# Attention's layer norm folded into centred query weights and a variance term, x brought in already transposed, and the opening in another order

## The chip, the cores and the metric
The kernel runs on one core of one Trainium2 chip. The metric is the device time in microseconds (us) of one execution; the time shown is the median of three runs. Engines are called as in the profile: PE is TensorE (PEld its weight loads), DVE is VectorE, ACT is ScalarE, POOL is GpSimd, SP issues DMAs.

## The reference
`x` is 4 batches of 512 tokens of width 512, the context as large. The attention has 32 heads of width 16, and each head's query and key are RMS-normed. The expert part has seven routed experts (two for each token) and a shared one.

```python
def _layernorm(x):                       # eps = 1e-5
    return (x - mean(x)) / sqrt(var(x) + eps)
q = _layernorm(x) @ Wq.T                 # 32 heads of 16
k, v = context @ Wk.T, context @ Wv.T    # rows interleaved in the reference
q, k = q * rsqrt(mean(q*q) + 1e-6), k * rsqrt(mean(k*k) + 1e-6)      # per head
x = x + softmax(q @ k.T / 4) @ v
x = x + experts(_layernorm(x))
```

## The kernel before
There are two blocks. The first is attention, with the second layer norm and the router's products beside it; the second is the expert part, over tiles of 256 tokens. Only the first is changed.

**Tiling.** Attention is worked in 16 units: 4 batches times 4 groups of 128 columns (8 heads). In code `u = 4 * b + g`. A unit has 8 steps: two halves of its heads (`ab`) times four tiles of 128 keys (`mt`). In a step PE makes the scores of four heads by 512 queries (`scored`, L322, four PSUM banks), ACT takes the exponential of all 2048 columns (L646), and PE weighs the values with it (`weighed`, L338). `scores` has one buffer, so the scores of a step wait for the exponential of the step before. Between the scores of step s and the weighing of step s-1, PE has other work that `between(u, s)` lists: the k projection of unit u+1 and u+2, the q projection of unit u+2, one 512-column group of v of the next batch (`v_all`), the head sums of squares (`sum_q`, `sum_k`, with the 0/1 matrix `blocks`), and transposes.

**Precision.** Each projection is done as three fp32r matmuls, high by high, high by low, low by high. So every operand is split: high is a copy to fp32r, low the difference. `weight_low`, `weight_split`, `context_split` and the functions for `xt` do this.

**The first layer norm.** For each tile of 128 tokens DVE takes mean and variance (`stat`, L668), POOL takes (variance + eps) to the power -0.5 (`root`, L181) and normalises the tile (`norm`, L211), PE transposes it (`four_transposes`, L405), and ACT and DVE split the transposed tile into `xt_hi` and `xt_lo` (L522, L705, L722, L723). Columns of `xt` are tokens, so q needs all four tiles. For a following batch these steps stand in groups 1 and 2: transposes of tile 0 and 1 in steps 5 and 6 of group 1, of tile 2 in step 0 and tile 3 in step 2 of group 2. In the first batch DVE normalises (L928) and the transposes go to the idle `scores` banks.

**The RMS norm.** DVE adds 16 * 1e-6 to the head sums (`sums_q` L752, `sums_k` L758), ACT takes log and exp(-0.5 *), DVE and POOL refine with one Newton step, and DVE stacks the result in pairs of heads (`stack_q` L794 to L796, `stack_k` L801 to L804).

**Order.** Every engine has its own queue, written out by hand. Three PSUM banks are shared out in a fixed order that the function `uses` writes down: `bank_a` (k, some v), `bank_b` (q, some v) and `tr` (sums, transposes, router). `begin` waits until DVE has read the bank's use before. DVE's order of a step is in `step(u, s)`, ACT's in `before_exp(u, s)`.

**Opening.** SP loads four tiles of x, then k's group 0, the context, q's group 0, v, and the rest. PE does half of k(0), 16 transposes, the rest of k(0), its sum, q(0), v(0,0), sum_q(0), v(0,1), v(0,3), q(1), five turns of k(1) and sum_q(1), then the first scores.

Of the kernel before, what the change touches and what calls it, by code (L numbers as in the profile page):

```python
# [12 lines left out]
P = 128  # L13


def moe_layer(nc, x, ctx_t, wq_t, wk_t, wv_t, w_all, b_up_gate, b_down, w_router, b_router, gate_bias, xn_dram,
# [20 lines left out]
    with ExitStack() as ctx:  # L37
# [49 lines left out]
        twin_hi = asb("twin_hi", [P, SEQ], FP32R)  # L87
# [5 lines left out]
        blocks = asb("blocks", [P, P])  # L93
        lower, sign = asb("lower", [P, 1]), asb("sign", [P, 1])
# [6 lines left out]
        x_first = [sem(f"x_first{t}") for t in range(BT)]  # L101
# [9 lines left out]
        xn_ready, first_t, xt_high, xt_split = (sem(n) for n in ("xn_ready", "first_t", "xt_high", "xt_split"))  # L111
# [26 lines left out]
        def uses(bank):  # L138
            order = {"a": [("k", 0), ("k", 1)], "b": [("q", 0), ("q", 1), ("v", 0, 2)],
                     "tr": [("sum_k", 0), ("sum_q", 0), ("sum_q", 1)]}[bank]  # L140
            for u in range(UNITS):
                b, g, more, behind = batch_of(u)
                ahead = u + 2 < UNITS
                if bank == "a":
                    order += [("v", b + 1, 2 * g - 3)] * (more and g >= 2) + [("t", b + 1, 0)] * (more and g == 1)
# [3 lines left out]
                else:  # L149
                    order += [("t", b + 1, 2)] * (more and g == 2) + [("l", b - 1, 2)] * (behind and g == 3)  # L150
                    order += [("out", u - 1, 1)] * (u > 0)
                    order += [("sum_k", u + 1)] * (u + 1 < UNITS) + [("t", b + 1, 3)] * (more and g == 2)
# [18 lines left out]
        def _(pool):  # L171
# [10 lines left out]

            nc.gpsimd.memset(blocks[:], 1.0).then_inc(blocks_set, 1)
# [19 lines left out]
            def norm(b, i):  # L203
                if i == 0:
                    pool.wait_ge(rsqrt_ready, (1, 2, 3, 5)[b])
                    pool.wait_ge(mean_ready, (1, 2, 3, 5)[b])
                elif i == 2:
                    pool.wait_ge(a_ready, A_AT["t", b, 0] + 1)
                elif i == 3:
                    pool.wait_ge(tr_ready, TR_AT["t", b, 1] + 1)  # L210
                nc.gpsimd.tensor_scalar(xn[:, i % 2, :], x_sb[:, tile_of(b, i), :], mv[:, i, 0:1], rsqrt[:, 0, i:i + 1],  # L211
                                        ALU.subtract, ALU.mult).then_inc(xn_ready, 1)

            def norm2(b, i):
                if i == 0:
                    pool.wait_ge(rsqrt_ready, (4, 6, 7)[b])
# [6 lines left out]
            root(0, 0)  # L223
# [3 lines left out]
            roots = 1  # L227
            for u in range(UNITS):
                b, g, more, behind = batch_of(u)
                if more and g == 1:  # L230
                    norm(b + 1, 0)
                    norm(b + 1, 1)
# [3 lines left out]
                if behind and g == 1:  # L236
                    root(roots, 1)
                    roots += 1
                    norm2(b - 1, 0)
                    norm2(b - 1, 1)  # L240
# [3 lines left out]
                if more and g == 1:  # L244
                    norm(b + 1, 2)
                    norm(b + 1, 3)
# [3 lines left out]
                if u == 0 or (g == GROUPS - 1 and b + 2 < BATCH):  # L250
                    root(roots, 0)
                    roots += 1

        @block.sync
        def _(sp):
# [20 lines left out]
            load_context(1)  # L276
            sp.wait_ge(zeros_set, 1)
            zeros = xt2[:, 1].rearrange("p c n -> p (c n)").unsqueeze(1)
            for rows, width in ((xn_dram, D), (out, D), (xn_dram[:, D:], WIDE - D)):
                spare = rows[TOKENS:, 0:width].rearrange("(s p) d -> p s d", p=P)  # L280
                sp.dma_start(spare, zeros[:, :, 0:width].to_broadcast([P, 2, width])).then_inc(y_filled, 16)
            for b in range(1, BATCH):
                sp.wait_ge(ctx_split, (b + 1) * MT)
                if b + 1 < BATCH:
                    load_context(b + 1)
                else:
# [4 lines left out]
                for i in range(BT):  # L291
                    t = tile_of(b - 1, i)
# [8 lines left out]
        def _(pe):  # L301
# [8 lines left out]
            def scored(u, s):  # L310
# [4 lines left out]
                if t:  # L315
                    pe.wait_ge(p_ready, t)
                else:
                    pe.wait_ge(v_ready, MT - 1)
                for part in (k_hi, k_lo):
# [31 lines left out]
            def q_turns(u, first, end):  # L351
                g = u % GROUPS
                if first == 0:
                    begin("b", B_AT, ("q", u), b_free)
                    pe.wait_ge(w_split, W_AT[f"q{g}"] + 1)
                    pe.wait_ge(xt_split, (u // GROUPS + 1) * BT)
                for c, a, b in TURNS[first:end]:
                    last = nc.tensor.matmul(bank_b[:], (wq_hi, wq_lo)[a][:, g, c, :], (xt_hi, xt_lo)[b][:, c, :],
# [5 lines left out]
            def k_turns(u, first, end):  # L364
                g = u % GROUPS
                if first == 0:
                    begin("a", A_AT, ("k", u), a_free)
                    pe.wait_ge(w_split, W_AT[f"k{g}"] + 1)
                    pe.wait_ge(ctx_split, (u // GROUPS + 1) * MT)
                for c, a, b in TURNS[first:end]:  # L370
                    last = nc.tensor.matmul(bank_a[:], (wk_hi, wk_lo)[a][:, g, c, :], (ctx_hi, ctx_lo)[b][:, c, :],
# [5 lines left out]
            def v_all(at, b, mt):  # L377
                pe.wait_ge(w_split, W_AT["v"] + 1)
                pe.wait_ge(ctx_split, b * MT + mt + 1)
# [28 lines left out]
            def norm_transposes(b, i):  # L408
                if i:
                    begin("tr", TR_AT, ("t", b, i), tr_free)  # L410
                    at, ready = tr, tr_ready
                else:
                    begin("a", A_AT, ("t", b, i), a_free)
                    at, ready = bank_a, a_ready
# [1265 lines left out]
```

## Time and profile before
| what | us |
|---|---|
| median of three runs (1018.45 to 1020.17) | 1018.86 |
| profiled execution, its own time | 1018.88 |
| its span | 1017.1 |
| PE busy | 960.4 |
| DVE busy | 703.6 |
| ACT busy | 498.4 |
| POOL busy | 230.6 |

The span is from the first to the last instruction of the profiled execution. Busy times overlap between engines. A matmul's end is modelled and matmuls are pipelined, so the distance between two starts tells more of PE's pace than a duration. In a timeline a row's bracket is the idle time of its engine just before it, and what ended it.

### The profile page before, as it was taken

How to read it: one execution, taken by the hardware profiler on the slowest of the kernel's cores; microseconds unless marked ns; L12 is line 12 of the kernel's file. 1: busy time of each engine (PE TensorE's matmuls, PEld its weight loads, DVE VectorE, ACT ScalarE, POOL GpSimd, SP SyncE). 2: the span in 40 equal slices, each digit the busy share in tenths (PEclk: the TensorE clock that was granted, in tenths of full speed). 3: DMA queues.
4: the chain of work that ended last, by engine and by line, in shares of the span. 5: the costliest groups of instructions: out<-in, count | busy, mean ns of one | idle time of the engine just before them, and what ended most of it. 6: DMA issues, size and time to landing. Idle time of an engine off the chain costs nothing.

```text
span 1017.1 us, 18058 instructions
## 1 busy us (share of the span) xinstructions
PE 960.4 (94%) x6730; PEld 698.0 (69%) x6731; DVE 703.6 (69%) x1442; ACT 498.4 (49%) x614; POOL 230.6 (23%) x223
## 2 busy tenths in 40 slices
PE   3999999999999999985999999999999999999995
PEld 3634443454444554332999999899998998999995
DVE  5788767876688657764579775765857677757653
ACT  3577668855786658875233222422424243424211
POOL 1122012420132201321000000232333332333321
PEclk9999999999999999998799999999999999999998
DMA  9100100010000100301341214363363535544523
GB/s 342 73 1 2 42 1 1 22 64 1 1 2 21 63 1 1 105 21 42 99 153 55 72 46 183 74 190 59 74 186 73 175 64 168 167 108 111 144 56 41
DMA packets 28985, 78.94 MB, mean 78 GB/s; under 512 B 7040, under 2 KB 7040, under 8 KB 24832
## 3 DMA queue, kind: packets, MB, share of 16 engines
q1 hardware_dynamic: 18400, 52.31, 14.4%
q0 software_dynamic: 10528, 25.87, 12.8%
q8 instruction: 36, 0.59, 0.2%
q14 instruction: 21, 0.17, 0.1%
HBM read 57.64 MB, written 20.52 MB: 77 GB/s over the span
## 4 chain that ended last, share of the span: by engine, by line
PE 49%; DVE 2%; issue 1%; DVEq 0%; POOL 0%; ACT 0%; POOLq 0%
PE u_ps L1188 16%; PE z_ps L1188 15%; PE y_ps L1188 15%; PE xt_ps L1201 2%; PE z_ps L1182 1%; DVE w_sb L1390 1%; PE y_ps L1214 0%; DVE stats L1406 0%; DVE u_lo L1551 0%; DVE x_lo L1400 0%; DVEq L1032 0%; DVE y_sb L1579 0%; POOL out L1132 0%; PE xt_ps L1174 0%; ACT u_hi L1322 0%
## 5 line engine op out<-in xcount | busy, mean ns | idle before, releaser
L646 ACT ACTIVATE probs<-scores 128x2048 f32<-128x2048 f32 x128 | 240.6, 1879 | 75.8 <-PE scores L322 72.8
L1188 PE MATMUL u_ps<-x_hi,w_sb 128*128 128x256 f32 x896 | 167.9, 285 | 5.2 <-issue 3.0
L1188 PE MATMUL z_ps<-u_hi,w_sb 128*128 128x256 f32 x896 | 169.1, 287 | 0.2 <-DVE u_lo L1551 0.2
L1188 PEld LDWEIGHTS u_ps<-x_hi,w_sb 128*128 128x128 f32 x896 | 143.1, 194 | 8.0 <-issue 4.6
L1322 ACT ACTIVATE u_hi<-u_ps,b_ug 128x256 fp32r<-128x256 f32 x112 | 47.0, 471 | 204.0 <-PE u_ps L1188 204.0
L1188 PEld LDWEIGHTS z_ps<-u_hi,w_sb 128*128 128x128 f32 x896 | 142.4, 193 | 0.4 <-DVE u_lo L1551 0.4
L1188 PE MATMUL y_ps<-w_sb,g_hi 128*128 128x512 f32 x448 | 138.8, 391 | 0.4 <-DVE g_lo L1569 0.4
L338 PE MATMUL o_ps<-probs,v_sb 128*17 128x512 f32 x1024 | 134.8, 598 | 1.0 <-ACT probs L646 1.0
L1188 PE MATMUL u_ps<-x_lo,w_sb 128*128 128x256 f32 x448 | 127.7, 285 | 0.0
L1188 PE MATMUL z_ps<-u_lo,w_sb 128*128 128x256 f32 x448 | 127.2, 284 | 0.0
L1551 DVE SCALAR_TENSOR_TENSOR u_lo<-u_ps,b_ug,u_hi 128x256 fp32r<-128x256 f32 x112 | 49.0, 479 | 80.7 <-ACT u_hi L1322 80.0
L322 PEld LDWEIGHTS scores<-q_st,k_hi 32*128 32x128 f32 x512 | 24.6, 181 | 112.6 <-ACT probs L646 67.8
L1334 ACT ACTIVATE s_sb<-z_ps,b_ug 128x256 f32<-128x256 f32 x112 | 47.0, 471 | 104.0 <-PE z_ps L1188 103.9
L1188 PEld LDWEIGHTS y_ps<-w_sb,g_hi 128*128 128x128 f32 x448 | 82.3, 188 | 16.3 <-issue 0.5
L1132 POOL DMA_INDIRECT out<-y_sb,target x42 | 69.3, 1650 | 101.7 <-DVE y_sb L1586 92.2
L1188 PEld LDWEIGHTS u_ps<-x_lo,w_sb 128*128 128x128 f32 x448 | 86.9, 194 | 0.9
L1188 PE MATMUL y_ps<-w_sb,g_lo 128*128 128x512 f32 x224 | 87.2, 389 | 0.0
L1188 PEld LDWEIGHTS z_ps<-u_lo,w_sb 128*128 128x128 f32 x448 | 86.4, 193 | 0.0
L1564 DVE SCALAR_TENSOR_TENSOR g_sb<-u_ps,b_ug,s_sb 128x256 f32<-128x256 f32 x112 | 53.8, 481 | 31.7 <-ACT s_sb L1334 31.5
L322 PE MATMUL scores<-q_st,k_hi 32*128 32x512 f32 x512 | 64.6, 494 | 7.1 <-ACT probs L646 6.8
L1308 ACT ACTIVATE w_sb<-w_raw 128x1024 fp32r<-128x1024 f32 x48 | 48.1, 1060 | 31.0 <-PE y_ps L1188 28.3
L1579 DVE TENSOR_TENSOR y_sb<-y_ps,bd 128x512 f32<-128x512 f32 x56 | 38.4, 685 | 29.2 <-PE y_ps L1188 29.1
(218 smaller groups left out, 1585.5 us busy)
## 6 DMA issues: line engine op xcount, KB each, us to landing
w_raw<-w_all SPq DMA_DIRECT2D x27, 1024.0 KB, 7.0
ctx_raw<-ctx_t SPq DMA_DIRECT2D x4, 1024.0 KB, 6.8
out<-x_sb SPq DMA_DIRECT2D x16, 256.0 KB, 2.0
xg<-xn_dram POOLq DMA_DIRECT2D x14, 256.0 KB, 3.1
x_sb<-x SPq DMA_DIRECT2D x1, 3072.0 KB, 18.1
xn_dram<-xn SPq DMA_DIRECT2D x12, 256.0 KB, 2.1
bd<-b_down SPq DMA_DIRECT2D x9, 256.0 KB, 4.2
x_sb<-x SPq DMA_DIRECT2D x4, 256.0 KB, 3.7
```

What stands on the lines that cost most here:

```text
L322: last = nc.tensor.matmul(scores[:, j, :], part[rows, u % 2, ab, mt * P:(mt + 1) * P], q_st[rows, u % 2, ab, :], start=(part is k_hi), sto ...
L338: last = nc.tensor.matmul(o_ps[32 * j:32 * j + HD + 1, :], v_sb[b % 2][:, mt, head, :], probs[:, t % 2, j, :], start=(mt == 0), stop=(mt = ...
L646: nc.scalar.activation(probs[:, t % 2], scores[:], ACT.Exp).then_inc(p_ready, 1)
L1132: nc.gpsimd.indirect_dma_start(out=out, in_=y_sb[:, h, :], in_offset=None, compute_op=ALU.add, out_offset=bass.IndirectOffsetOnAxis(ap=tar ...
L1188: ins = nc.tensor.matmul(out_ps, stat[a], mov[b], start=(first and a + b == 0), stop=(last and a == 1), skip_group_check=True)
L1201: last = nc.tensor.transpose(xt_ps[:, b, a, h * P:(h + 1) * P], xg[:, h, c * P:(c + 1) * P], ident[:])
L1308: nc.scalar.activation(w_sb[:, par, 0, m, two], w_raw[:, m, two], ACT.Copy).then_inc(hi_done, 1)
L1322: last = nc.scalar.activation(u_hi[:, c, :], u_ps[:, b, a, :], ACT.Identity, bias=b_ug[:, par, 0, c:c + 1])
L1334: nc.scalar.activation(s_sb[:, c, :], z_ps[:, b, a, :], ACT.Silu, bias=b_ug[:, par, 1, c:c + 1]).then_inc(s_done, 1)
L1551: nc.vector.scalar_tensor_tensor(u_lo[:, c, :], u_ps[:, b, a, :], bias[:, c:c + 1], u_hi[:, c, :].bitcast(FP32), ALU.add, ALU.subtract)\
L1564: nc.vector.scalar_tensor_tensor(g_sb[:, c, :], u_ps[:, b, a, :], bias[:, c:c + 1], s_sb[:, c, :], ALU.add, ALU.mult).then_inc(g_done, 1)
L1579: nc.vector.tensor_tensor(at, y_v[:, h, :], bd[:, par, :], ALU.add).then_inc(y_done, 1)
```

## The change
- The host hands over `x_t`, x transposed and in the layout of `ctx_t`: 4 chunks of 128 columns of x, each by 512 tokens.
- `xt_hi` and `xt_lo` are split from raw x, chunk by chunk (`x_high`, `x_low`, `x_split`), out of `xn[:, 0:2]` in SBUF, where SP loads the chunks two at a time (`load_x`). POOL's `norm`, PE's `norm_transposes` and the root for this norm are gone. A group-0 q projection waits for the chunk that its turn needs.
- The mean is taken out through the weights: for each group PE multiplies raw query weights with a matrix of 1/512 (`weight_means`) and the result is subtracted, by DVE for group 0 and by POOL for groups 1 to 3 (`centre`).
- The variance is not divided out. Since the RMS norm follows, it scales that norm's epsilon only: PE spreads the variances along a row (`eps_rows`, four fp32 matmuls of the broadcast variance column with the identity into `tr`), DVE makes `eps = 16e-6 * variance + 16e-11` (`eps_out`), and `sums_q` adds this tile. `eps_rows` of the next batch stands in group 2, step 6.
- `stack_q` writes its high part into `q_st` and subtracts in place; `twin_hi` is gone.
- The opening has another order: loads k(0), context, q(0), x_t in two halves, x in two halves, v. PE: means of q(0), k(0), half of q(0), sum of k, rest of q(0), eps rows, means of groups 1 to 3, sum_q(0), then v(0,0), v(0,1), v(0,3) as before. DVE takes its statistics after the sum of k, and splits v after the sum of q.

```diff
@@ uses
-                     "tr": [("sum_k", 0), ("sum_q", 0), ("sum_q", 1)]}[bank]
+                     "tr": [("sum_k", 0), ("eps", 0), ("sum_q", 0), ("sum_q", 1)]}[bank]
-                    order += [("out", u, 0)] + [("t", b + 1, 1)] * (more and g == 1)
+                    order += [("out", u, 0)] + [("eps", b + 1)] * (more and g == 2)
@@ gpsimd
+            def centre(g, raw):
+                nc.gpsimd.tensor_tensor(raw, raw, wmean[:, g, :].unsqueeze(1).to_broadcast([P, DC, P]), ALU.subtract)\
+                  .then_inc(q_centred, 1)
...
+            pool.wait_ge(wmean_read, 1)
+            centre(1, q_raw[:, 1])
+            for g in range(EARLY, GROUPS):
+                centre(g, q_raw2[:, g - EARLY])
...
-                    norm(b + 1, 0)
-                    norm(b + 1, 1)
@@ sync
-            for t in range(BT):
-                sp.dma_start(x_sb[:, t, :], x_v[:, t, :]).then_inc(x_first[t], 16)
+            def load_x(b, c):
+                sp.dma_start(xn[:, c % 2, :], x_t[b, :, c]).then_inc(xt_loaded[c % 2], 16)
+
             sp.dma_start(k_raw[:, 0], wk_t[:, 0]).then_inc(w_loaded["k0"], 16)
             load_context(0)
             sp.dma_start(q_raw[:, 0], wq_t[:, 0]).then_inc(w_loaded["q0"], 16)
+            for h in range(2):
+                sp.dma_start(xn[:, 2 * h:2 * h + 2, :], x_t[0, :, 2 * h:2 * h + 2]).then_inc(xt_first[h], 16)
+            for h in range(2):
+                sp.dma_start(x_sb[:, 2 * h:2 * h + 2, :], x_v[:, 2 * h:2 * h + 2, :]).then_inc(x_first[h], 16)
             sp.dma_start(v_raw[:], wv_t).then_inc(w_loaded["v"], 16)
...
+            def rest_of_x(b):
+                for c in range(2, DC):
+                    sp.wait_ge(xt_split, b * DC + c - 1)
+                    load_x(b, c)
@@ tensor
+            def eps_rows(b):
+                begin("tr", TR_AT, ("eps", b), tr_free)
+                pe.wait_ge(var_known, b + 1)
+                for t in range(BT):
+                    last = nc.tensor.matmul(tr[:, t * P:(t + 1) * P], mv[:, t, 1:2].to_broadcast([P, P]), ident[:],
+                                            start=True, stop=True, skip_group_check=True)
+                last.then_inc(tr_ready, 1)
+
+            def weight_means(groups):
+                for g in groups:
+                    raw = q_raw[:, g] if g < EARLY else q_raw2[:, g - EARLY]
+                    for c in range(DC):
+                        last = nc.tensor.matmul(scores[:, 2, g * P:(g + 1) * P], share, raw[:, c, :], start=(c == 0),
+                                                stop=(c == DC - 1), skip_group_check=True)
+                last.then_inc(wmean_ready, 1)
...
                 elif s == 6:
-                    if more and g == 1:
-                        norm_transposes(b + 1, 1)
+                    if more and g == 2:
+                        eps_rows(b + 1)
                     if behind and g == 2:
                         gates(b - 1, 0)
...
-            k_turns(0, 0, 6)
-            for i in range(BT):
-                pe.wait_ge(xn_ready, i + 1)
-                four_transposes(scores[:, i, :], xn[:, i, :]).then_inc(first_t, 1)
-            k_turns(0, 6, 12)
+            pe.wait_ge(share_set, 1)
+            pe.wait_ge(w_loaded["q0"], 16)
+            weight_means((0,))
+            k_turns(0, 0, 12)
+            q_turns(0, 0, 6)
             sum_k(0)
-            q_turns(0, 0, 12)
+            q_turns(0, 6, 12)
+            eps_rows(0)
...
+            weight_means((1, 2, 3))
+            sum_q(0)
             v_all(scores[:, 0, :], 0, 0).then_inc(first_v, 1)
-            sum_q(0)
@@ scalar
+            def x_high(b, c):
...
+                nc.scalar.activation(xt_hi[:, c, :], xn[:, c % 2 if b else c, :], ACT.Copy).then_inc(xt_high, 1)
...
+            act.wait_ge(q0_centred, 1)
             high("q0", wq_hi[:, 0], q_raw[:, 0], 0)
@@ vector
+            def x_split(b, c):
+                dve.wait_ge(xt_loaded[c % 2], 16 * (2 * b - 1 + c // 2))
+                raw = xn[:, c % 2, :]
+                done(nc.vector.tensor_copy(xt_hi[:, c, :], raw))
...
+            def eps_out(b):
+                take_tr(("eps", b))
+                done(nc.vector.tensor_scalar(eps[:], tr[:], HD * RMS_EPS, HD * RMS_EPS * LN_EPS, ALU.mult, ALU.add))
                 dve.sem_inc(tr_free)
...
-                done(nc.vector.tensor_scalar(ssq[:], tr[:], HD * RMS_EPS, None, ALU.add))
+                done(nc.vector.tensor_tensor(ssq[:], tr[:], eps[:], ALU.add))
...
             sums_k(0)
-            weight_low("v", wv_lo[:], v_raw[:], wv_hi[:])
+            dve.wait_ge(x_first[0], 16)
+            stat(0, mv[:, 0, :])
+            stat(1, mv[:, 1, :])
             first_root_k(0)
+            dve.wait_ge(x_first[1], 16)
+            stat(2, mv[:, 2, :])
+            stat(3, mv[:, 3, :])
+            ask_eps()
             newton_k(0)
+            eps_out(0)
+            sums_q(0)
...
+            low.then_inc(w_split, 1)
+            first_root_q(0)
             stack_k(0, 0)
-            sums_q(0)
```

## Rows read from the trace of the kernel before

**Rows 1.** The page, busy us of each engine (share of the span).
```profile
PE 960.4 (94%) x6730; PEld 698.0 (69%) x6731; DVE 703.6 (69%) x1442; ACT 498.4 (49%) x614; POOL 230.6 (23%) x223
```

**Rows 2.** Windows of attention: us, busy PE, PEld, DVE, ACT, POOL, clock, DMA.
```profile
152.00:266.00 114.00, 111.50 (x774) 52.99 (x771) 84.73 (x164) 78.92 (x68) 27.91 (x18) 1.00 0.06 20
```

**Rows 3.** Waits, 45 to 440 us: total us, times, longest.
```profile
ACT probs L646 <- PE scores L322: 62.3, 66, 3.4
PEld scores L322 <- ACT probs L646: 57.2, 67, 1.3
```

**Rows 4.** Timeline of PE, opening: start, us, line, out<-in, [idle before <-releaser].
```profile
26.90 0.50 PE L345 MATMUL scores<-wv_hi,ctx_hi 128*128 128x512 f32 x1 [0.53 <-DVE wv_lo L679]
...
40.97 0.50 PE L322 MATMUL scores<-q_st,k_hi 32*128 32x512 f32 x4
```

**Rows 5.** Timeline of ACT, group 1, batch 0 and batch 3: exponentials of steps 5, 6, 7.
```profile
81.80 1.88 ACT L646 ACTIVATE probs<-scores 128x2048 f32<-128x2048 f32 x1
...
85.22 1.88 ACT L646 ACTIVATE probs<-scores 128x2048 f32<-128x2048 f32 x1 [0.52 <-PE scores L322]
88.59 1.89 ACT L646 ACTIVATE probs<-scores 128x2048 f32<-128x2048 f32 x1 [1.49 <-PE scores L322]
...
416.50 1.88 ACT L646 ACTIVATE probs<-scores 128x2048 f32<-128x2048 f32 x1
...
419.48 1.88 ACT L646 ACTIVATE probs<-scores 128x2048 f32<-128x2048 f32 x1 [0.62 <-PE scores L322]
422.26 1.88 ACT L646 ACTIVATE probs<-scores 128x2048 f32<-128x2048 f32 x1 [0.89 <-PE scores L322]
```

**Rows 6.** Timeline around group 2, step 2 of batch 0: ACT, PE, DVE.
```profile
97.81 1.88 ACT L646 ACTIVATE probs<-scores 128x2048 f32<-128x2048 f32 x1 [0.35 <-PE scores L322]
...
106.30 1.88 ACT L646 ACTIVATE probs<-scores 128x2048 f32<-128x2048 f32 x1 [0.55 <-PE scores L322]
...
99.11 0.50 PE L345 MATMUL bank_b<-wv_hi,ctx_hi 128*128 128x512 f32 x1 [1.35 <-DVE qn L764]
...
103.94 0.66 PE L405 MATMUL tr<-ident,xn 128*128 128x128 f32 x4 [0.94 <-DVEq L759]
...
95.56 1.05 DVE L795 CAST twin_hi<-twin 128x512 fp32r<-128x512 f32 x1
...
103.13 0.69 DVE L758 TENSOR_SCALAR ssk<-tr 128x512 f32<-128x512 f32 x1 [0.27 <-PE tr L394]
```

**Rows 7.** Timeline of PE: router products of 7 columns; a sum of 512 columns.
```profile
226.54 1.95 PE L428 MATMUL tr<-wr,xt 128*128 128x7 f32 x16
...
40.02 1.02 PE L389 MATMUL tr<-sq,blocks 128*128 128x512 f32 x2
```

**Rows 8.** Timeline of the opening: ACT's first copies, DVE's statistics and splits, k at its start.
```profile
9.07 0.63 ACT L519 ACTIVATE wk_hi<-k_raw 128x512 fp32r<-128x512 f32 x1 [6.94 <-DMA k_raw<-wk_t]
11.62 2.19 ACT L621 ACTIVATE ctx_hi<-ctx_raw 128x512 fp32r<-128x512 f32 x4 [1.92 <-DMA ctx_raw<-ctx_t]
...
3.60 0.69 DVE L668 BATCH_NORM_STATS2 stats<-x_sb 128x6 f32<-128x512 f32 x1 [3.48 <-DMA x_sb<-x]
...
12.28 2.50 DVE L688 TENSOR_TENSOR ctx_lo<-ctx_raw,ctx_hi 128x512 fp32r<-128x512 f32 x4 [1.78 <-ACT ctx_hi L621]
...
24.55 2.29 DVE L679 TENSOR_TENSOR wv_lo<-v_raw,wv_hi 128x2048 fp32r<-128x2048 f32 x1 [0.24 <-DVE ssk L758]
...
15.49 0.63 PE L371 MATMUL bank_a<-ctx_lo,wk_hi 128*128 128x512 f32 x1
...
15.92 0.63 PE L371 MATMUL bank_a<-ctx_hi,wk_lo 128*128 128x512 f32 x1
```

**Rows 9.** Start of the expert part: PE's timeline, then windows as in rows 2.
```profile
478.35 1.97 PE L1201 MATMUL xt_ps<-ident,xg 128*128 128x128 f32 x8 [5.33 <-DMA xg<-xn_dram]
...
483.50:486.90 3.40, 3.40 (x18) 3.40 (x18) 2.07 (x2) 1.24 (x2) 0.07 (x1) 0.50 0.92 225
...
493.70:497.10 3.40, 3.40 (x19) 3.40 (x19) 1.31 (x3) 0.00 (x0) 0.00 (x0) 0.51 0.41 154
```

More of the change, by code:

```diff
@@ L99, in moe_layer @@
         tr = ps("tr", [P, 512])
[L101 removed]
+        x_first = [sem(f"x_first{t}") for t in range(2)]
+        xt_first = [sem(f"xt_first{t}") for t in range(2)]
+        xt_loaded = [sem(f"xt_loaded{t}") for t in range(2)]
+        share_set, wmean_ready, wmean_read, q0_centred, q_centred = (
+            sem(n) for n in ("share_set", "wmean_ready", "wmean_read", "q0_centred", "q_centred"))
         x_rest, r_loaded = sem("x_rest"), sem("r_loaded")
@@ L144, in uses @@
                 if bank == "a":
-                    order += [("v", b + 1, 2 * g - 3)] * (more and g >= 2) + [("t", b + 1, 0)] * (more and g == 1)
+                    order += [("v", b + 1, 2 * g - 3)] * (more and g >= 2)
                     order += [("k", u + 2)] * ahead
@@ L149, in uses @@
                 else:
-                    order += [("t", b + 1, 2)] * (more and g == 2) + [("l", b - 1, 2)] * (behind and g == 3)
+                    order += [("l", b - 1, 2)] * (behind and g == 3)
                     order += [("out", u - 1, 1)] * (u > 0)
-                    order += [("sum_k", u + 1)] * (u + 1 < UNITS) + [("t", b + 1, 3)] * (more and g == 2)
+                    order += [("sum_k", u + 1)] * (u + 1 < UNITS)
                     order += [("l", b - 1, 0), ("l", b - 1, 1)] * (behind and g == 2)
                     order += [("l", b - 1, 3), ("gates", b - 1, 2)] * (behind and g == 3)
-                    order += [("out", u, 0)] + [("t", b + 1, 1)] * (more and g == 1)
+                    order += [("out", u, 0)] + [("eps", b + 1)] * (more and g == 2)
                     order += [("gates", b - 1, 0)] * (behind and g == 2) + [("sum_q", u + 2)] * ahead
@@ L285, in _ @@
                     load_context(b + 1)
+                    for c in range(2):
+                        sp.wait_ge(xt_split, b * DC + c + 3)
+                        load_x(b + 1, c)
                 else:
@@ L291, in _ @@
                 for i in range(BT):
+                    if i == 2 and b + 1 < BATCH:
+                        rest_of_x(b + 1)
                     t = tile_of(b - 1, i)
@@ L437, in between @@
                 if s == 0:
-                    if more and g == 2:
-                        norm_transposes(b + 1, 2)
                     if behind and g == 3:
@@ L450, in between @@
                         sum_k(u + 1)
-                    if more and g == 2:
-                        norm_transposes(b + 1, 3)
                 elif s in Q_TURNS:
@@ L465, in between @@
                         out_transposes(u, 0)
-                        if more and g == 1:
-                            norm_transposes(b + 1, 0)
                         if more and g >= 2:
@@ L594, in before_exp @@
                         square_k(u + 1)
+                    if more and g == 2:
+                        x_high(b + 1, 3)
                 elif s == 3:
-                    if more and g == 2:
-                        norm_high(b + 1, 3)
                     if nxt:
@@ L618, in _ @@
             act.wait_ge(ctx_loaded, 16)
-            for mt in range(MT):
-                keys = slice(mt * P, (mt + 1) * P)
-                nc.scalar.activation(ctx_hi[:, :, keys], ctx_raw[:, :, keys], ACT.Copy).then_inc(ctx_high, 1)
+            for c in range(DC):
+                nc.scalar.activation(ctx_hi[:, c, :], ctx_raw[:, c, :], ACT.Copy).then_inc(ctx_high, 1)
+            act.wait_ge(q0_centred, 1)
             high("q0", wq_hi[:, 0], q_raw[:, 0], 0)
-            for i in range(BT):
-                act.wait_ge(first_t, i + 1)
-                xt_high_out(scores[:, i, :], i)
+            for c in range(DC):
+                x_high(0, c)
             square_k(0)
-            high("v", wv_hi[:], v_raw[:], 0)
             log_k(0)
@@ L630, in _ @@
             square_q(0)
+            act.wait_ge(w_loaded["v"], 16)
+            for h in range(2):
+                two = slice(2 * h, 2 * h + 2)
+                nc.scalar.activation(wv_hi[:, two, :], v_raw[:, two, :], ACT.Copy).then_inc(w_high, 1)
+            act.wait_ge(wmean_ready, 2)
+            nc.scalar.copy(wmean[:, 1:], scores[:, 2, P:].rearrange("p (g n) -> p g n", n=P)).then_inc(wmean_read, 1)
+            log_q(0)
+            root_q(0)
+            act.wait_ge(q_centred, 1)
             high("q1", wq_hi[:, 1], q_raw[:, 1], 1)
@@ L894, in step @@
                 elif s == 6:
+                    if more and g == 2:
+                        eps_out(b + 1)
                     if more and g == 1:
-                        norm_low(b + 1, 0)
-                        norm_both(b + 1, 1)
+                        x_low(b + 1, 0, DC + 2 * b + 1)
+                        x_split(b + 1, 1)
                     if nxt:
```

168 lines of the change are left out of this document (73 added, 95 removed).

## The prediction
> **What bounds the kernel now.** I read the page first: TensorE (PE) is busy for 94% of a 1017.1 us span [rows 1], and more than half of that span is the expert part, which the change does not touch. Then the busy time by stage [rows 2]. Attention runs from the first exponential at 41.76 to about 475 us. In the second batch's 114 us PE is busy for 111.5, but not all of that is at its peak: [rows 3] shows two waits of the same size, ScalarE (ACT) for scores (62.3 us) and PE for ACT's exponential (57.2 us). So I read attention step by step, by the starts of its 128 exponentials. A plain step takes 2.71 us: exponential, then scores, which have one buffer. A step in which PE has more than that to do between two scores is longer, and there the PE queue sets the time. The changed instructions stand in just such steps. Before 41.76 is the opening: DMA, then a chain through all engines, and from 26.90 to 40.97 a PE queue without a hole [rows 4]. So there are two sums: batches, and opening. Vector engine (DVE) and Pool count only where PE waits for them.
>
> **Batches: what goes.** Each of three coming batches has 16 transposes of its normalised rows.
> Two tiles fall in group 1, steps 5 and 6. Steps 5 and 6 of batch 0 take 3.42 and 3.37 us (exponentials from 81.8 over 85.22 to 88.59), those of batch 3, which has no following batch, 2.98 and 2.78 (416.50, 419.48, 422.26) [rows 5]. The gain is 0.44 + 0.59 = 1.03 a batch: four transposes and the start of what follows. The ACT copy that replaces the one from PSUM costs the same 0.6 us beside the scores.
> One tile falls in group 2, step 0, as full for PE as step 5 above: 0.43 a batch.
> The last is in group 2, step 2, the dearest step: 97.81 to 106.30, 8.49 us [rows 6]. In it PE waits 1.35 us for bank_b, because DVE is late with qn; after the sums it waits 0.94 us for tr, since DVE must read the k sums before the transposes may write there, and then transposes. In the new kernel the transposes and the second wait go: v 2.76 to 2.87, sums 0.95, weighing 0.98, scores 0.7: about the 5.46 us between the exponentials of the same step in group 3. The first wait shrinks: DVE no longer waits 0.19 for transposes, splits out of SBUF (0.43, as for the context) instead of PSUM (0.69), and its cast at 95.56 took 1.05 instead of 0.43 us while Pool normalised a tile, work that is gone. That is 1.07 us earlier, with PE ready 0.4 earlier, so 0.7 of the 1.35 stay. New step: about 6.2, gain 2.3. With 0.14 in step 3 the gains are 1.03 + 0.43 + 2.3 + 0.14 = 3.9 a batch, 11.7 in all.
>
> **Batches: what comes.** eps_rows is four fp32 matmuls of 128 columns in group 2, step 6, a step that PE fills (117.18 to 119.97). No row has this shape. From below: sixteen records (eight fp32 matmuls of 7 columns) take 1.88 us, 0.235 each; from above, half of a 512-column one, 0.95/2. I take 0.24, near the first since a quarter of 0.95 is 0.24 too: 0.95 a batch (0.94 to 1.9), 2.85 in all. For two of the three batches the router matmuls follow at once in the same bank, so PE now waits until DVE has copied the eps row: 0.13 + 0.69 + 0.1 = 0.92, twice, 1.84 [rows 7]. Behind that wait stand the weighing, four k matmuls and the next scores, all of the path. Last, DVE's order is unchanged, but PE reaches step 3 sooner than DVE does, by about 1.2 us of lag; in batch 0 DVE's idle time in steps 5 and 6 absorbs it, in the two batches with tiles of the second norm the transposes of o_sb wait for the bank, 0.75 each: 1.5. Balance: -11.7 + 2.85 + 1.84 + 1.5 = **-5.5 us**; bounds -8 (no lag, smaller first wait) and -2.
> Free: 12 Pool normalisations (Pool idles), the variance added in sums_q (a two-tensor read of PSUM takes DVE 0.69, as the scalar form does), the 12 chunk loads of 256 KB (each has some 5 us between the split that frees its buffer and its use; if one were late it would hold DVE and q by some 2 us), SP's queue (chunks 2 and 3 wait in it for splits, behind them two stores of the second norm, which only the expert part reads), stack_q with its high part in place (same three instructions). Pool's centring of the other weights is due 8 us before PE asks for q1.
>
> **Opening.** Where does the last wait end now? v begins at 26.90, after wv_lo; the PE queue from there is 14.07 us, with one sum_q (0.95) in it. In the new order sum_q(0) comes before v, so 13.1 us stand behind v's split, and all hangs on when DVE has made wv_lo. I follow it [rows 8].
> - Landing. Before, k0 is the last of the first 1.31 MB asked for and is there at 9.07, the context ends 2.36 MB and is there at 11.62. Now q0 ends 1.57 MB: on the same curve 9.7, with large packets first perhaps 8.7. I take 8.9.
> - Column means of q0: four fp32 matmuls on a PE that starts at half rate (its first 512-column matmuls come every 0.43 us, later 0.23): 1.7 to 1.9, to 10.7. Centring 0.69, then two context lows (0.62 each), q0 low 0.7, four x lows 2.6: DVE at 16.0. Nothing waits for a norm here.
> - sum_k ends at 16.9; k sums 0.7; two tiles of statistics 1.9; first root 0.7; two more tiles 1.9: variances known at 22.3. Before, all this sat ahead of 8.3, in DMA time; now it is on the path.
> - PE: eps rows 0.95, twelve fp32 matmuls for the other column means 2.85, sum_q 0.95: 27.1.
> - DVE: q sums 0.8 and wv_lo in two halves 2.4: 30.4.
> Then 13.1: first scores at 43.5 to 43.9 against 40.97: **+2.9**, of which 2.85 are the means of groups 1 to 3 put ahead of sum_q(0). What goes, 16 transposes (2.75), DVE's four norms (1.9) and the root on Pool, lay before 22 us and is already out of this sum. All other engines are earlier: stack_q(0,0) would be ready near 36.5 where 40.5 is wanted.
> - The clock. In this chain PE stands idle from about 18 to 22.3 and again some 3 us before v. [Rows 9]: at the start of the expert part PE idled 5.3 us to 478.35 and its granted clock reads 0.50, 1.2 GHz, even while PE is wholly busy from 483.50 to 486.90; it is 0.51 again in the stretch from 493.70. So each new hole may be followed by work at half rate. A busy stretch like that from 483.50 does in its 3.40 us what full rate does in 1.70. I take one such loss, 1.7: **+4.6**. Bounds: +1 (data early, no drop) to +9.
> The Trainium skill, "TensorE: Matmul & The Clock Gate", section "HAM oscillation", says that a PE made to wait between bursts falls back to half rate and pays the return each time. By that rule both holes would pay; by the opening before, where the PE queue kept its pace from 26.90 on behind a hole of 0.5 us [rows 4], a short hole costs nothing. The trace agrees with the rule for the longer holes.
>
> **Sum.** The profiled execution took 1018.88, its span 1017.1, and the median is 1018.86, so no correction: 1018.9 - 5.5 + 4.6 = **1018.0**. A change under 0.2%, 2.0 us, is no change here.
>
> **Rivals.**
> A, the opening costs little: no drop of the clock, +2.9 or less, and DVE's lag is absorbed in all batches, -7.0: 1014.8. For it: a short hole kept the clock [rows 4], and one of the two here may fall so that it counts little. Against: both are over 3 us.
> B, the opening turns into the bound: slower. Its place is the PE queue ahead of v, where eps_rows and the weight means behind it wait for DVE's statistics; price 2.9 and 1.7 for each of the two holes, 1.2 for landings on the old curve, and 1.0 if PE stays at half rate for a stretch longer at its start: +8.5, less 5.5: 1021.9. It decides from an opening of +7.5, first scores at 48.5. For it: rows 9. Against: large packets go first.
> C, the 8.49 us step keeps its length, since log_k waits for DVE's k sums whatever PE does, and its 2.3 are not gained: batches -5.5 + 3 x 2.3 = +1.4, opening +4.6: 1024.9. For it: ACT's log stands ahead of the next exponential. Against: the k sums were done at 103.82, 2.5 us before the exponential.
>
> **How the numbers follow.** Forecast case 0.42 (its own range 1016 to 1020), A 0.30, B 0.20, C 0.08. Faster by over 0.2%: A and a fifth of the forecast case, 0.38; slower: B, C but for their lower edge, and a little of the forecast case, 0.27; same 0.35. The range of 8 in 10 runs from 1013.5 to 1022.5: the rest of B, most of C and an A with a better opening are left out.
>
> **What would show it.** The first exponential: 45 to 46.5 for the forecast, 44.3 for A, over 48 for B; half-rate stretches or 0.43 us between v matmuls; PE idle before eps_rows about 4 us. Group 2, step 2 at 6.2 us, steps 5 and 6 of group 1 at 2.98 and 2.78, group 2 step 6 longer by 0.95 (batch 0) and 1.87 (batches 1 and 2). From the last exponential on, as before. Wrong if the new first exponential comes before 42, if the dear step stays over 8 us, or if DVE waits for an x chunk.

## The result, and the profile after
| | before | after |
|---|---|---|
| median of 7 runs each, us | 1018.86 (1017.63 to 1020.17) | 1024.3 (1022.45 to 1026.25) |
| profiled execution, its span | 1018.88, 1017.1 | 1024.3, 1022.6 |
| first exponential, last exponential | 41.76, 468.62 | 48.57, 473.61 |

The ratio is 1.0054 [1.0043, 1.0066]: slower, where 1018.0 was forecast, and above the range. Between the marks of the last row the traces differ by +6.81 (opening), -1.82 (batches) and +0.46 (all behind), 5.45 in all. Forecast were +4.6 and -5.5. Two executions among the experiments, 1348 us (e4_eps_after) and 3400 us (a run of the kernel before), were disturbed and no ratio counts them.

The page of the kernel after, busy times and the two lines that matter, against [rows 1]; the digits are 40 equal slices:
```profile
PE 967.1 (95%) x6730; PEld 702.7 (69%) x6731; DVE 705.3 (69%) x1440; ACT 498.7 (49%) x616; POOL 208.3 (20%) x211
...
PE   5899999999999999985899999999999999999995
...
PEclk9899999999999999999699999999999999999998
```
POOL has lost the normalisations of the first norm (230.6 to 208.3). PE has as many instructions and is busy 6.7 us longer. The second digit of PEclk is 8: the clock fell in the opening. The windows of the opening say where (columns as in [rows 2]):
```profile
20.80:27.60 6.80, 5.16 (x24) 5.19 (x25) 3.41 (x7) 0.70 (x1) 0.00 (x0) 0.50 1.05 389
27.60:34.40 6.80, 3.42 (x18) 2.37 (x18) 4.50 (x7) 1.74 (x3) 2.54 (x2) 1.00 0.98 374
34.40:37.90 3.50, 3.50 (x10) 2.69 (x10) 3.46 (x3) 1.74 (x3) 3.50 (x3) 0.51 0.08 21
```
PE's timeline of the same stretch:
```profile
7.98 2.05 PE L440 MATMUL scores<-q_raw,xt 128*128 128x128 f32 x8 [7.98 <-DMA q_raw<-wq_t]
...
22.44 2.05 PE L432 MATMUL tr<-ident,mv 128*128 128x128 f32 x8 [4.13 <-DVEq L701]
24.28 4.44 PE L440 MATMUL scores<-q_raw,xt 128*128 128x128 f32 x24
28.56 1.02 PE L409 MATMUL tr<-sq,blocks 128*128 128x512 f32 x2
32.97 0.50 PE L361 MATMUL scores<-wv_hi,ctx_hi 128*128 128x512 f32 x1 [3.38 <-DVE wv_lo L975]
...
35.31 0.63 PE L361 MATMUL scores<-wv_hi,ctx_lo 128*128 128x512 f32 x1
35.73 0.63 PE L361 MATMUL scores<-wv_hi,ctx_hi 128*128 128x512 f32 x1
```
Both forecast holes are there, 4.13 and 3.38 us, and work at half rate stands at each. From 22.44 to 28.56 four eps products and twelve means take 6.1 us (3.8 in the forecast), and v's matmuls start 0.43 us apart from 34.46 to 37.87, against 0.23 behind the short hole of [rows 4].

Group 2 of the first batch on ACT, the steps of [rows 6]; the dear step is from 103.14 to 109.54, then step 6, from 121.04 to 124.89 (3.85 us, 2.79 before):
```profile
103.14 1.89 ACT L672 ACTIVATE probs<-scores 128x2048 f32<-128x2048 f32 x1
108.83 0.63 ACT L577 ACTIVATE r<-ssk 128x512 f32<-128x512 f32 x1 [3.80 <-DVEq L782]
109.54 1.88 ACT L672 ACTIVATE probs<-scores 128x2048 f32<-128x2048 f32 x1
...
121.04 1.88 ACT L672 ACTIVATE probs<-scores 128x2048 f32<-128x2048 f32 x1 [3.35 <-PE scores L338]
124.89 1.88 ACT L672 ACTIVATE probs<-scores 128x2048 f32<-128x2048 f32 x1 [1.98 <-PE scores L338]
```
The same group of the second batch on PE, step 6, where [rows 7] stood at 226.54, and the window behind it:
```profile
228.32 1.16 PE L432 MATMUL tr<-ident,mv 128*128 128x128 f32 x8
230.32 1.95 PE L454 MATMUL tr<-wr,xt 128*128 128x7 f32 x16 [0.84 <-DVEq L747]
232.20 1.75 PE L354 MATMUL o_ps<-probs,v_sb 128*17 128x512 f32 x8
...
234.90 0.63 PE L391 MATMUL bank_a<-ctx_hi,wk_lo 128*128 128x512 f32 x1
```
```profile
232.40:235.80 3.40, 3.40 (x12) 1.17 (x4) 0.11 (x2) 0.00 (x0) 0.00 (x0) 0.50 0.00 0
```
The wait for the eps copy is there (0.84), and behind the router's products comes what nobody forecast: 3.4 us at half rate with PE wholly busy. The step from exponential to exponential takes 8.23 us there and 6.66 at the same place of the third batch, where the clock stays at full rate: the stretch costs 1.57.

**Low time.** Each run lists its mean granted clock; with half and full rate as the only levels, (1 - clock) x 2 x span is the time that the record shows at half rate. PE's start is not in it: in the kernel after the clock reads 1.00 from 7.98 us on, though the 512-column matmuls come 0.43 us apart until 13.67. Before: mean low time 30.6 us over 55 runs beside the experiments, 39 of them at 28.4 or 28.5. After: 42.7 over 7. The difference, 12 us, is worth 6 us of work if PE sets the time in all of it; that is the highest price. Over the seven runs of the kernel after the time rises by only 0.34 us for each us of low time (1022.45 at 38.8, 1026.25 at 49.2), which gives 4 us. Each run's time less half its low time is 1003.4 in the mean before and 1002.9 after. So apart from the clock the change is worth between -0.5 and +1.4 us.

### The profile page after: what moved, and what is told of

The parts are those of the page before. It is cut to its first block, busy times and chain, and to the rows that moved or that the text cites. A ratio compares the mean times of both kernels' runs of the same rounds, so it can differ in the third digit from the quotient of the medians.

```text
span 1022.6 us, 18034 instructions
## 1 busy us (share of the span) xinstructions
PE 967.1 (95%) x6730; PEld 702.7 (69%) x6731; DVE 705.3 (69%) x1440; ACT 498.7 (49%) x616; POOL 208.3 (20%) x211
## 4 chain that ended last, share of the span: by engine, by line
PE 49%; DVE 2%; issue 1%; DVEq 0%; POOL 0%; ACT 0%; POOLq 0%
PE u_ps L1229 15%; PE z_ps L1229 15%; PE y_ps L1229 15%; PE xt_ps L1242 2%; PE z_ps L1223 1%; DVE w_sb L1431 1%; PE y_ps L1255 0%; DVE stats L1447 0%; DVE u_lo L1592 0%; DVE x_lo L1441 0%; DVEq L1073 0%; DVE y_sb L1620 0%; POOL out L1173 0%; PE xt_ps L1215 0%; ACT u_hi L1363 0%
## 5 line engine op out<-in xcount | busy, mean ns | idle before, releaser
L204 POOL TENSOR_TENSOR r<-r 128x512 f32<-128x512 f32 x16 | 18.0, 1123 | 228.6 <-ACT r L587 228.6
```

The source lines that it names most:

```text
L204: nc.gpsimd.tensor_tensor(r2[:], r0[:], r0[:], ALU.mult).then_inc(r2q_ready, 1)
```

## The experiments
The clock theory: the slowdown is the granted clock, in the two holes of the opening and behind the router's products in the batches. The order theory: it is late data and DVE's order, at any clock. The new-code theory: what the change adds brings the half-rate stretches of the batches. "First exp" is the first exponential; edits are on the kernel after, if not said otherwise.

With the same opening the eps rows start up to 1.5 us apart from trace to trace, so first exponentials are compared from the start of the eps rows (us). e4_eps_after and e6_no_eps leave the opening as it is in the kernel after, and are two more traces of it:

| trace | eps rows | v | first exp | eps rows to first exp |
|---|---|---|---|---|
| after | 22.44 | 32.97 | 48.57 | 26.13 |
| e4_eps_after | 21.60 | 31.15 | 46.75 | 25.15 |
| e6_no_eps | 20.91 | 30.59 | 46.21 | 25.30 |
| e1_fill | 23.92 | 31.98 | 46.98 | 23.06 |
| e2_means_early | 22.34 | 28.82 | 44.45 | 22.11 |
| e3_v_first | 21.00 | 26.71 | 47.44 | 26.44 |
| e7_open_only | 19.88 | 25.61 | 39.89 | 20.01 |
| e5_best | 19.43 | 24.90 | 38.94 | 19.51 |

**e1_fill**: both holes filled with products of no use.
```diff
+            keep_busy(16)
             eps_rows(0)
...
             sum_q(0)
+            keep_busy(13)
             v_all(scores[:, 0, :], 0, 0).then_inc(first_v, 1)
```


> The changed kernel with two fills on TensorE in its opening: 16 matmuls of 512 columns (about 3.7 us) before eps_rows(0) and 13 (about 3.0 us) after sum_q(0), into a scores bank that v overwrites later. Nothing else moves. Theory (half clock after the holes): the granted clock stays 1.00 to the first exponential, eps rows and weight means take about 0.95 + 2.85 us instead of 1.84 + 4.28, v's matmuls keep 0.23 us; first exponential 48.57 - 2.3 - 1.6 = 44.7, time about 1020.4. Rival (the fp32 shape itself costs 0.36 us a matmul, and v slows for another reason): eps rows and means keep 6.1 us, first exponential stays near 48.6, time 1024.3.

1022.38 (1018.28 to 1025.27, 6 runs), ratio 1.0024 [1.0001, 1.0048]. PE's timeline and a window of it:
```profile
23.92 1.13 PE L437 MATMUL tr<-ident,mv 128*128 128x128 f32 x8 [0.48 <-DVEq L708]
24.89 2.84 PE L445 MATMUL scores<-q_raw,xt 128*128 128x128 f32 x24
27.57 1.02 PE L409 MATMUL tr<-sq,blocks 128*128 128x512 f32 x2
```
```profile
20.00:31.90 11.90, 11.09 (x63) 8.79 (x61) 8.58 (x16) 4.72 (x7) 2.07 (x2) 1.00 1.04 392
```
The same twelve means take 2.68 us from start to next start instead of 4.28, the clock reads 1.00, and from the eps rows to the first exponential it takes 23.06 us, against 26.13, 25.15 and 25.30 in the three traces with the holes. So the holes do cost rate, and it is not the fp32 shape that is slow: 3.1 us in the trace of the kernel after, 2.1 and 2.2 in the two others. It is less than the 3.9 that was expected, since a wait for DVE comes out behind v:
```profile
41.24 0.47 PE L375 MATMUL bank_b<-xt_hi,wq_hi 128*128 128x512 f32 x1 [0.81 <-DVE wq_lo L715]
```
The profiled run had three stretches at half rate in the batches (230.5, 346.5, 448.9), where the kernel after had one (232.4), and from first to last exponential it took 2.65 us more. Two of the six runs had a low time of 28.5 us, as most runs of the kernel before, and took 1018.28 and 1018.64.

**e2_means_early**: the means of groups 1 to 3 in the first hole.
```diff
+            weight_means((1, 2, 3))
             eps_rows(0)
-            weight_means((1, 2, 3))
```


> The weight means of groups 1 to 3 stand before eps_rows(0), in the hole in which TensorE waits for the variances. Theory (they are on the path only through their place): they run in the hole as soon as q2's weights are there, sum_q(0) ends about 4.3 us earlier, v starts near 29 instead of 32.97, and the first exponential is at 44 to 45 (43 if the second hole no longer drops the clock), time about 1020. Rival (q2's weights land late, near 22 us, or the clock falls all the same): the gain is 1 us or less, 1023.5.

1026.03 (1023.27 to 1027.75, 4 runs), 1.0070 [1.0045, 1.0095]. First exp 44.45, 4.1 us earlier than after, with the eps rows at the same time, as expected; and yet the time is no better: stretches at half rate of 20.5 us in all fell in the batches and the opening, against 13.7 in the trace of the kernel after. Low time 50.2; time less half of it 1000.7, 2.2 better. The reorder gains; the clock hides it.

**e3_v_first**: DVE splits v before it takes the sums of q.
```diff
-            sums_q(0)
             for h in range(2):
...
             split_count[0] += 2
+            sums_q(0)
```


> VectorE splits the v weights before it takes the q sums, in its 4.3 us of idle time before them. Theory: v's matmuls follow sum_q(0) at once, at 29.5 instead of 32.97, and without the second hole the clock does not fall a second time: first exponential 48.57 - 3.4 - 1.6 = 43.6, time about 1019.3. Rival (the q chain through log, root and stacking becomes the last, or the clock falls anyway): first exponential 45 to 47, time 1021 to 1023.

1025.48 (1022.31 to 1027.54, 6 runs), 1.0059 [1.0040, 1.0078]. The hole before v is gone, but from the eps rows to the first exponential it takes 26.44 us, 0.3 more than in the kernel after: a wait took its place, and behind it PE works at half rate from 38.0 to 44.8.
```profile
39.01 0.77 PE L375 MATMUL bank_b<-xt_hi,wq_hi 128*128 128x512 f32 x1 [3.54 <-DVE wq_lo L708]
```
DVE reaches that split only at 38.18, behind the stacking of group 0, in which three operations take 1.23, 1.67 and 1.78 us; POOL centres weights from 30.56 to 34.98. The same forms take 0.49, 0.75 and 0.69 us elsewhere. The last of the three stands behind POOL's work in e5_best, whose edit follows below, and takes 0.68 there (the first two, still beside POOL, take 1.22 and 1.67). DVE and POOL of e3_v_first, then of e5_best:
```profile
33.75 1.78 DVE L793 TENSOR_TENSOR r<-ssq,r 128x512 f32<-128x512 f32 x1
30.56 4.42 POOL L223 TENSOR_TENSOR q_raw<-q_raw,o_sb 128x512 f32<-128x512 f32 x3
```
```profile
32.41 0.68 DVE L793 TENSOR_TENSOR r<-ssq,r 128x512 f32<-128x512 f32 x1
28.02 2.72 POOL L223 TENSOR_TENSOR q_raw<-q_raw,o_sb 128x512 f32<-128x512 f32 x2
```
The first exponential is 1.1 us earlier than in the kernel after only because the variances were known 1.4 us earlier in this trace. So moving the split of v alone gains nothing: the order theory holds for the opening as well as the clock theory.

**e4_eps_after**: eps rows behind the weighing, router's products first.
```diff
-                    if more and g == 2:
-                        eps_rows(b + 1)
                     if behind and g == 2:
...
+                if s == 6 and more and g == 2:
+                    eps_rows(b + 1)
```
`uses` has the same order, and eps_out goes to step 7.

> For the batches that follow, eps_rows stands behind the router products and the weighing of group 2, step 6, not ahead of the router products; VectorE makes the eps row in step 7. Theory: the 0.84 us wait goes in two batches, and the half-rate stretch of batch 1 from 232.4 us goes with it: step 6 of batches 1 and 2 at 5.8 instead of 8.23 and 6.66; 0.9 + 0.9 + 1.6 = 3.3 us less, time about 1021. Rival (the half-rate stretch is set by the router's narrow matmuls, not the wait): only 1.8 us less, 1022.5.

1021.97 (1017.86 to 1024.12 and one at 1348, 10 runs), 1.0027 [1.0008, 1.0045]. Group 2 of the second batch takes 34.41 us instead of 37.09: the wait (0.84) and the half-rate stretch there (1.57) are gone. But a stretch came in the next group (33.05 instead of 31.49) and one in group 2 of the third batch (342.2 to 345.6), and low time is the same, 42.8. Time less half of it is 999.8, 3.1 better than after: the order gains, and which batch has a stretch changes with it.

**e6_no_eps**: no steady eps_rows and eps_out; batches 1 to 3 use batch 0's eps row, so this part of the result is left out.
```diff
-                    order += [("out", u, 0)] + [("eps", b + 1)] * (more and g == 2)
+                    order += [("out", u, 0)]
```
The two calls go with it.

> The changed kernel without eps_rows and eps_out for batches 1 to 3 (they keep the row of batch 0, so their RMS epsilon is that of other tokens). It prices the row in the batches. Theory (the eps row costs its matmuls, VectorE's answer and, with the narrow router products, a stretch of half clock): group 2, step 6 back to 2.79 and 4.65, 5.0 us less plus the half-rate stretches beyond the opening's, about 1.6 to 3: 1017 to 1018, mean low time 39 us. Rival (the half-rate stretches in the batches come without the row too): 5.0 us less and no more, 1019.

1017.8 (1015.37 to 1019.35, 12 runs), 0.9991 [0.9982, 1.0000]. Group 2 takes 29.49, 33.50, 33.47 us, against 30.59, 37.09, 35.55 after: the row costs 1.1 in the first batch, 2.1 in the third, 2.0 and a stretch in the second. Low time is still 42.7, with such a stretch again behind router products:
```profile
438.06 1.95 PE L454 MATMUL tr<-wr,xt 128*128 128x7 f32 x16 [0.16 <-DVEq L835]
...
441.38 0.64 PE L338 MATMUL scores<-q_st,k_lo 32*128 32x512 f32 x4
```
```profile
437.70:441.10 3.40, 3.24 (x32) 2.17 (x32) 3.13 (x9) 1.88 (x1) 0.00 (x0) 1.00 0.22 80
441.10:444.50 3.40, 3.18 (x20) 0.80 (x24) 3.22 (x7) 1.88 (x1) 0.00 (x0) 0.50 0.00 0
```
The time, 1017.8, lies in the range that was expected if the row brings the stretches (1017 to 1018), the low time does not (39 us was expected then). The stretches decide: that speaks against the new-code theory, since without the new row they come too, at the router's products, which the change did not touch.

**e8_shift7, e9_shift14**: the kernel *before*, with n products of no use ahead of the first scores, n = 7 and 14, so that all the rest stands later by 1.05 us in the first trace and 2.58 in the second, and nothing of the change is in it.
```diff
             sum_q(1)
+            keep_busy(n)
             pe.wait_ge(r_loaded, 48)
```


> The kernel before with seven 512-column matmuls of no use (their result is overwritten) in the opening, just ahead of the first scores, where the PE queue has no hole. All that follows is the code before, 7 x 0.237 = 1.66 us later: nothing of the change is in it. Theory P (where the router products fall against the edges of the clock's stretches decides whether a half-rate stretch follows them, so that any shift of the kernel can bring one): one or more stretches at 0.50 of 3.4 us within the batches, right behind a group of router products (group 2 step 6 or group 3 step 4), where the kernel before shows none; low-clock time from 30 to about 40 us; time 1018.9 + 1.7 + 5 = 1024 to 1026. Theory R (the new code makes the clock fall, and the shift does nothing): no stretch below full rate between 45 and 475 us, 1018.9 + 1.7 = 1020.5.

> The same with fourteen such matmuls, 14 x 0.237 = 3.32 us, nearly the 3.4 us between two edges of the clock's stretches in the traces so far, so that the router products fall against the edges as they do in the kernel before. Theory P: no half-rate stretch in the batches, low-clock time back at about 30 us, time 1018.9 + 3.3 = 1022.2, thus below the run with seven although it does more. Theory R: the same 1022.2, but then 1.7 above the run with seven. A theory by which any shift brings stretches gives 1026 or more.

With seven: 1022.13 (1019.92 to 1023.77, 12 runs), 1.0031 [1.0020, 1.0042], low time 34.0. With fourteen: 1022.01 (1019.46 to 1024.36, 10 runs), 1.0031 [1.0019, 1.0044], low time 31.2. PE and window of the first, then of the second:
```profile
227.57 1.95 PE L433 MATMUL tr<-wr,xt 128*128 128x7 f32 x16
229.45 1.34 PE L338 MATMUL o_ps<-probs,v_sb 128*17 128x512 f32 x8
230.72 0.80 PE L376 MATMUL bank_a<-ctx_hi,wk_hi 128*128 128x512 f32 x1
231.32 0.63 PE L376 MATMUL bank_a<-ctx_lo,wk_hi 128*128 128x512 f32 x1
```
```profile
226.60:230.10 3.50, 3.50 (x36) 2.30 (x32) 2.33 (x6) 1.88 (x1) 0.00 (x0) 1.00 0.29 119
230.10:233.50 3.40, 3.40 (x16) 1.67 (x12) 0.00 (x0) 0.00 (x0) 0.00 (x0) 0.50 0.00 0
```
```profile
229.11 1.95 PE L433 MATMUL tr<-wr,xt 128*128 128x7 f32 x16
230.99 1.05 PE L338 MATMUL o_ps<-probs,v_sb 128*17 128x512 f32 x8
231.98 0.50 PE L376 MATMUL bank_a<-ctx_hi,wk_hi 128*128 128x512 f32 x1
232.31 0.39 PE L376 MATMUL bank_a<-ctx_lo,wk_hi 128*128 128x512 f32 x1
```
```profile
230.10:233.50 3.40, 3.40 (x29) 1.98 (x28) 1.05 (x3) 1.02 (x1) 0.00 (x0) 1.00 0.01 2
```
The unchanged code, 1 us later, gets the stretch of the kernel after, at the same place, and behind 3.50 us in which PE had no idle time; 1.5 us later still, it does not. So position alone brings one. Each is one trace, but the runs agree: none of the twelve with seven has a low time of 28.4 or 28.5 us, five of the ten with fourteen have, and 39 of the 55 of the kernel before. The size was less than expected: the seven cost 2.0 us beyond their 1.7, not 5; the fourteen 0.2 beyond their 3.3, as expected. The two medians are equal although one does half as much. Time less half the low time is 1004.9 and 1006.4, against 1003.3 for the runs of the kernel before beside them: 1.65 and 3.15 more, close to the 1.66 and 3.32 that were put in.

**e7_open_only, e5_best**: a better opening alone, then with the eps row moved. The opening: v's split before the sums of q (e3); two tiles of statistics before sums_k(0) and two before the first root; the splits of q1 and k1 ahead of newton_q(0); POOL centres group 1 before root2_q(0). e5_best adds e4's edit, and norm2_out(b - 1, 0) goes before context_split(b + 1, 3).
```diff
-            sums_k(0)
             dve.wait_ge(x_first[0], 16)
             stat(0, mv[:, 0, :])
             stat(1, mv[:, 1, :])
-            first_root_k(0)
+            sums_k(0)
             dve.wait_ge(x_first[1], 16)
...
             stack_k(0, 0)
+            weight_low("q1", wq_lo[:, 1], q_raw[:, 1], wq_hi[:, 1])
+            weight_low("k1", wk_lo[:, 1], k_raw[:, 1], wk_hi[:, 1])
             newton_q(0)
             stack_q(0, 0)
```


> Only the opening's new order of e5_best, batches as in the changed kernel. Theory: the first exponential at 38 to 39.5 as in e5_best, no half rate before it, time 1024.3 less 9 to 10: 1014.5 to 1015.5. Rival (the gain of an earlier start is given back later, as VectorE or the loads are then late in unit 0): the first two units longer than 25.6 and 23.1, time over 1017.

> The changed kernel with another opening and another group 2. Opening: VectorE takes two tiles of statistics before the k sums and the others right after, splits v before the q sums and q1, k1 before the Newton step; Pool centres group 1 before it squares q's root. Batches: eps_rows behind the weighing of step 6, the first tile of the second norm read from its bank before the last context split. Theory (order, and the clock as its consequence): variances known at about 20 us, v starts near 25, no TensorE hole over 2 us is left, so no half rate before the first exponential; it comes at 38 to 39.5 (before: 41.76, changed: 48.57). Batches 1 and 2, group 2, near 33.8. Apart from the clock 3 us below the kernel before in the opening and 4 to 5 in the batches: 1011 to 1013. Rival (half rate in the batches is bound to this region whatever the order): first exponential as said, but 4 to 8 us more low clock in the batches, 1014 to 1017.

e7_open_only: 1015.9 (1013.59 to 1018.75, 5 runs), 0.9971 [0.9953, 0.9990], first exp 39.89. e5_best: **1013.71** (1011.84 to 1016.19, 6 runs), 0.9953 [0.9936, 0.9970]; it beats the kernel before and, by 10.6 us, the one after. Its opening on PE, and the windows of opening and batches:
```profile
19.43 1.13 PE L432 MATMUL tr<-ident,mv 128*128 128x128 f32 x8 [2.56 <-DVEq L701]
20.40 2.84 PE L440 MATMUL scores<-q_raw,xt 128*128 128x128 f32 x24
23.08 1.02 PE L409 MATMUL tr<-sq,blocks 128*128 128x512 f32 x2
24.90 0.50 PE L361 MATMUL scores<-wv_hi,ctx_hi 128*128 128x512 f32 x1 [0.80 <-DVE wv_lo L974]
```
```profile
0.00:38.94 38.94, 27.92 (x132) 21.61 (x134) 29.09 (x51) 16.21 (x28) 9.35 (x19) 1.00 0.84 311
38.94:462.89 423.95, 412.81 (x2877) 186.52 (x2881) 305.88 (x590) 306.65 (x254) 62.41 (x46) 0.99 0.08 27
```
Variances 3.0 us earlier, holes of 2.56 and 0.80 us and no half rate: first exp 38.94, 9.6 before that of the kernel after. Group 2 takes 30.46, 34.20 and 34.21 us. It still pays for stretches in the batches (246.5, 437.7, 454.7 us), so low time is 38.8, and the time lies between what was expected without them (1011 to 1013) and with them (1014 to 1017). e7_open_only, with the same opening, had a hole of 1.90 us and a half-rate stretch from 19.92 to 23.34, against its expectation, e5_best a hole of 2.56 and none. Of e5_best's two additions the moved eps row brings most: group 2 of the later batches takes 35.5 us without a stretch in e7_open_only and 34.41 in e4_eps_after, which has the eps row's move alone; both moves give 34.2.

## Why the prediction was wrong
**What held.** The gains of the batches: group 1 gave 1.03 in each, as worked out; step 0 of group 2 0.43, step 3 0.15, the dear step 2.07 (6.40 long) instead of 2.3. The eps row's own cost was 1.07 (0.95), the wait behind it 0.84 (0.92). In the opening, variances were known at 22.24 (22.3), and both holes were where they were forecast. C's place is refuted, the dear step did shrink. x chunks were never late, and SP shows in no wait.

**The step that failed: "I take one such loss, 1.7".** Both holes paid, in this trace (20.8 to 27.6 and 34.4 to 37.9 at half rate) and in the two others of the same opening. Counted at PE, the first cost 2.3 here, since means and eps rows ran in its stretch nearly whole, the second 1.6: 3.9 for 1.7, which makes +6.8 of +4.6. Without the half rate e1_fill's 23.06 us behind the eps rows at 22.44 would give a first exponential at 45.50, +3.7: so the clock's share is 3.1, and the sum without it, 2.9 (the upper end of its 43.5 to 43.9), was 0.8 short.

Those 0.8 are DVE's order behind v, the wait for wq_lo of 0.81: "All other engines are earlier" failed there, as stack_q(0,0) was ready at 41.5 instead of 36.5, with three operations beside POOL's centring, costed at nothing, 2.6 us longer than elsewhere.

That both holes pay was rival B's rule, and its sign of a first exponential over 48 came true; its opening of +7.5 did not. Part of it is the draw of one trace: with the same opening the first exponential stood at 46.75 (e4_eps_after) and 46.21 (e6_no_eps), beside the forecast's 45 to 46.5.

The Trainium skill, "TensorE: Matmul & The Clock Gate", section "HAM oscillation", would have had both holes pay; the trace after agrees in these two, and e1 shows it by filling them. The page's case has waits that are longer than the 2 us of work between them and come each time; for a single hole e5's 2.56 us without a loss and e7's 1.90 us with one show no rule by its length.

**What was missing: the clock in the batches.** They were priced at full rate, as [rows 2] shows it with 1.00, and the sum has no term for a loss there. The kernel after lost 1.57 in its second batch. [rows 2] was true of one position of the router's products only, as e8 and e9 show.

**Terms mis-sized.** DVE's lag was 1.2 in each of the two later batches instead of 0.75; for part of that time DVE itself is slower (a context low at 217.76 took 1.41 instead of 0.69, while POOL squared a root from 217.41 to 218.63). With the dear step and the eps row this is 2.1 over the three batches. So the miss of 6.3 us is, by the traces, 1.4 (clock, opening) + 0.8 (DVE behind v) + 1.6 (clock, batches) + 2.1 (lag and waits) + 0.5 behind the last exponential, 6.4.

**What stays open.** What the clock costs the change is known only within bounds: 4 to 6 us by the low time of all runs, 4.6 by the one trace with e1_fill as the measure (3.1 and 1.6). How the chip decides where a stretch falls was only bracketed (e8, e9), and low time differs from run to run of one kernel (28.4 to 40.8 before). No run takes POOL's centring away, so that it slows DVE is argued from where the two overlap: the same operation takes 1.77 us beside it and 0.68 behind it. No cause is known for the 0.5 us behind the last exponential.

## What to carry to other kernels
When a change leaves holes in PE's queue, price all work behind each hole at half rate until a measured row says otherwise, and move independent PE work into the hole only with an eye on DVE's order. Where PE's clock falls in one position and not in another, a shift alone can cost as much as an edit brings (2.0 us in e8_shift7): compare low time per run beside the medians, and look at time less half the low time, which treats all low time as if PE set the time in it. Move statistics and splits that open a PE queue ahead of what nobody waits for; here the opening's order was worth 8.4 us (e7_open_only against the kernel after), 4.9 of them in time less half the low time.

## What the runs showed of the hardware
- An fp32 product of 128 columns takes 0.22 to 0.24 us at full rate (e1_fill: twelve in 2.68, four in 0.97) and 0.43 to 0.46 at half rate (the kernel after: four in 1.70 from 7.98 on, four in 1.84 from 22.44 on). The clock column does not show the first of these: it reads 1.00 before 20.8 us.
- The granted clock fell behind router products of 7 columns with PE busy for 3.50 of 3.50 us ahead of it (e8_shift7), and did not where the same code stood 1.5 us later (e9_shift14).
- A hole of 1.90 us was followed by half rate (e7_open_only) and one of 2.56 was not (e5_best), in the same code: the hole's length alone doesn't decide.
- While POOL worked through three operations of 128x512 (4.42 us), DVE's of the same size took 1.23 to 1.78 us instead of 0.49 to 0.75 (e3_v_first). The third of them takes 1.77 us beside POOL's work in the kernel after, and 0.68 where it starts behind POOL's last operation (e5_best, e7_open_only). No run takes POOL's work away.
